# Keeping q, k and v of a sequence in SBUF, with the projection weights streamed from DRAM: a transformer layer on eight cores

## The reference

```python
x = x + _layernorm(attn(_layernorm(x), cos, sin, wq, bq, wk, wv, bv, wo, bo))
x = x + _layernorm(ffn(_layernorm(x), w1, conv_w, conv_b, w2))

# attn: 16 heads of 64
q = x @ wq + bq;  k = x @ wk;  v = x @ wv + bv
q, k = rope of the last 1024 tokens of q and k, in bfloat16
out = softmax(q k^T / 8) v;  return out @ wo + bo
# ffn: hidden size 4096, weights quantized to -1, 0, 1 and activations to 8 bits
h = bit_linear(x, w1); h = silu(depthwise_conv(h, conv_w) + conv_b); return bit_linear(h, w2)
```

## Time and profile before

| | |
|---|---|
| timed runs | 5171.26 and 5133.98 us, median 5152.62 |
| profiled execution | 5104.38 us |
| its span on the slowest core (core 7) | 5102.8 us, 42393 instructions |
| spans of the 8 cores | 5071.9 to 5102.8 us |
| mean granted TensorE clock, by core | 0.826 to 0.829 |
| busy share of the span | PE 58%, weight loads 21%, DVE 40%, ACT 38%, POOL 3% |
| DMA | 343.42 MB, mean 67 GB/s |

### The profile page before, as it was taken

One profiled execution on the slowest core, in us unless ns is written; L12 is line 12 of the kernel. 1 busy time (PEld: TensorE's weight loads), 2 busy tenths in 40 slices (PEclk: granted clock), 3 DMA queues, 4 the chain that ended last, 5 costly groups with the idle time before them and its releaser, 6 DMA issues. The chain is left out here.

```text
span 5102.8 us, 42393 instructions; the slowest of 8 cores (5071.9 to 5102.8 us)
## 1 busy us (share of the span) xinstructions
PE 2950.4 (58%) x12366; PEld 1065.1 (21%) x12366; DVE 2023.0 (40%) x3238; ACT 1943.1 (38%) x2427; POOL 139.3 (3%) x246
## 2 busy tenths in 40 slices
PE   0000456678876331455788886331887788177577
PEld 0000222112211111222112211110332333033233
DVE  3334311244545444222244545444444344343433
ACT  0001344767775122344767765111222122242422
POOL 0000000000000000000000000000000000100000
PEclk9999988888987665788778888665998899588788
DMA  8574000100000222100100000223111111423232
GB/s 260 194 251 135 32 38 38 50 15 30 15 17 2 76 66 79 38 37 32 44 15 29 15 17 3 67 76 124 42 50 42 62 47 49 144 75 109 90 116 70
DMA packets 140105, 343.42 MB, mean 67 GB/s; under 512 B 42405, under 2 KB 75237, under 8 KB 135782
## 3 DMA queue, kind: packets, MB, share of 16 engines
q1 hardware_dynamic: 108330, 206.18, 12.1%
q0 software_dynamic: 31552, 134.53, 7.8%
HBM read 218.87 MB, written 117.60 MB: 66 GB/s over the span
## 5 line engine op out<-in xcount | busy, mean ns | idle before, releaser
L692 ACT ACTIVATE ptil<-sc,negM 128x1024 bf16<-128x1024 f32 x1024 | 1054.8, 1142 | 366.0 <-PE sc L623 365.1
L703 PE MATMUL accA<-ptil,dch 128*65 128x512 bf16 x1024 | 453.2, 443 | 154.9 <-DVE tmpB L722 153.9
L620 PE MATMUL sc<-qch,kch 64*128 64x512 bf16 x1024 | 423.5, 414 | 71.1 <-DMA dch<-vd_sp 24.5
L623 PE MATMUL sc<-qch,kch 64*128 64x512 bf16 x1024 | 434.0, 424 | 0.0
L705 PE MATMUL accB<-ptil,dch 128*65 128x512 bf16 x1024 | 430.6, 421 | 0.0
L1172 PE MATMUL p2a<-w2q,ring 128*128 128x512 bf16 x1024 | 241.1, 399 | 184.1 <-DVE outt L1189 159.0
L715 DVE COPY lbufA<-accA 1x512 f32<-1x512 f32 x64 | 43.8, 685 | 633.2 <-PE accB L705 633.2
L998 ACT ACTIVATE hsb<-pcA,convb_s 128x512 bf16<-128x512 f32 x128 | 88.0, 687 | 519.6 <-PE pcA L989 513.9
L157 ACT ACTIVATE stat<-stat 128x1 f32<-128x1 f32 x128 | 25.9, 203 | 675.7 <-DVE stat L152 675.6
L965 PE MATMUL pwA<-xqd,w1q 128*128 128x512 bf16 x1024 | 245.1, 382 | 44.6 <-DVE hsc L974 44.6
L861 PE MATMUL pw<-ident,xqtm 128*128 128x128 bf16 x256 | 32.4, 307 | 390.3 <-DVE xqtm L852 390.3
(11 more groups left out here) (215 smaller groups left out, 4557.2 us busy)
## 6 DMA issues: line engine op xcount, KB each, us to landing
xr<-x SPq DMA_DIRECT2D x64, 512.0 KB, 4.7
hs_sp<-hsb SPq DMA_DIRECT2D x64, 512.0 KB, 2.6
ring<-hs_sp SPq DMA_DIRECT2D x8, 4096.0 KB, 16.3
wstg<-w1t SPq DMA_DIRECT2D x4, 4096.0 KB, 15.9
wstg<-w1t POOLq DMA_DIRECT2D x4, 4096.0 KB, 24.5
wstg<-w2t SPq DMA_DIRECT2D x4, 4096.0 KB, 18.9
wstg<-w2t POOLq DMA_DIRECT2D x4, 4096.0 KB, 28.3
x_sp<-x2t SPq DMA_DIRECT2D x32, 512.0 KB, 2.7
```

Source lines behind the costliest of these rows:

```text
L620: TE.matmul(sc[sl][:, 0:512], kc_[0:64, kt * 128:(kt + 1) * 128], qc_[0:64, qc * 512:(qc + 1) * 512], start=True, stop=True, tile_position ...
L623: smmv[g] = st.inc(TE.matmul(sc[sl][:, 512:1024], kc_[64:128, kt * 128:(kt + 1) * 128], qc_[64:128, qc * 512:(qc + 1) * 512], start=True, ...
L692: expv[pl] = ss.inc(S.activation(ptil[pl][:], sc[sl][:], AF.Exp, bias=negM[:, p:p + 1], scale=1.0))
L703: TE.matmul(accA[:], dc4[:, kt, 0:65], ptil[pl][:, 0:512], start=(kt == 0), stop=(kt == NKT - 1))
```

## The change

The attention stage no longer reads q, k and v from DRAM. They stay in SBUF for a whole sequence (`qres`, `kres`, `vres`, 32 KB + 32 KB + 32.5 KB per partition), and ACT, DVE and rope write there directly. The three DRAM buffers, the seven spills of each block, the waits for them at its end and the loads in the attention stage are gone.

The space comes from three places. `w3` (48 KB per partition) is gone: in the setup DVE casts each batch of wq, wk and wv into `wqa` or `wqb`, and G spills it with four DMAs to `wqkv_sp`, which is laid out by column block; from there the QKV stage loads the weights of one block (768 KB) at a time into `wsb0` and `wsb1`, the next block's at the start of each block. The staging buffers are half as wide, so `quant_weight` makes 8 batches of 2 MB of each pass. In the Wo stage `ln3t`, `ln2t`, `qx16` and `xqtm` have one buffer each. The `xr` buffers are allocated per stage, as many as are used.

```diff
+    wqkv_sp = nc.dram_tensor("wqkv_sp", [OC, 128, 3 * KC * 128], BF16,
+                             kind="Internal").ap()
-        w3 = w3_es.enter_context(nc.sbuf_tensor(_un("w3"), [128, 3 * KC * H], BF16))
+        qres = w3_es.enter_context(nc.sbuf_tensor(_un("qres"), [128, OC * T], BF16))
+        kres = w3_es.enter_context(nc.sbuf_tensor(_un("kres"), [128, OC * T], BF16))
+        vres = w3_es.enter_context(
+            nc.sbuf_tensor(_un("vres"), [128, NPAIR * NKT * 130], BF16))
...
-        wstg0 = _ph.enter_context(nc.sbuf_tensor(_un("wstg0"), [128, 2 * DH], F32))
+        wstg0 = _ph.enter_context(nc.sbuf_tensor(_un("wstg0"), [128, DH], F32))
...
                 dstg[i % 2].wait(V, lv)
+                if i >= 2:
+                    dss[i % 2].wait(V, wspill[i % 2])
                 castv.append(sv.inc(V.tensor_copy(
-                    w3[:, (wh * KC + b * 4) * H:(wh * KC + b * 4 + 4) * H],
-                    stg[i % 2][:, 0:4 * H])))
+                    wqx[i % 2][:, 0:4 * H], stg[i % 2][:, 0:4 * H])))
+                sv.wait(G, castv[-1])
+                for k4 in range(4):
+                    tix = wh * KC + b * 4 + k4
+                    wspill[i % 2] = dss[i % 2].inc(G.dma_start(
+                        wqkv_sp[:, :, tix * 128:(tix + 1) * 128].rearrange(
+                            "o p n -> p o n"),
+                        wqx[i % 2][:, k4 * H:(k4 + 1) * H].rearrange(
+                            "p (o n) -> p o n", n=128)), 16)
...
-                nb = 2 * DH // width
+                nb = DH // width
...
+                    wldv[0] = dstg[0].inc(SY.dma_start(wsb[0][:], wqkv_sp[0]), 16)
                     for oc in range(OC):
                         par = oc % 2
-                        if oc >= 2:
-                            dsq[par].wait(S, spq[par])
-                            dsk[par].wait(S, spk[par])
-                            dsd[par].wait(V, spd[par])
+                        if oc + 1 < OC:
+                            sl2 = (oc + 1) % 2
+                            eng = SY if sl2 == 0 else G
+                            st.wait(eng, wsuse[sl2])
+                            wldv[sl2] = dstg[sl2].inc(
+                                eng.dma_start(wsb[sl2][:], wqkv_sp[oc + 1]), 16)
+                        dstg[par].wait(TE, wldv[par])
...
                             rolast = sv.inc(V.tensor_tensor(
-                                ro[:, ridx * 512:(ridx + 1) * 512], rt1[:], rt2[:],
-                                op=OP.add))
+                                src, rt1[:], rt2[:], op=OP.add))
...
-                        dsq[par].inc(G.dma_start(qf_sp[s, oc][:, 0:1024], qcb[par][:, 0:1024]), 16)
...
-                        spd[par] = dsd[par].inc(G.dma_start(vd_sp[s, oc], db[par][:]), 16)
-                        if oc < OC - 1:
-                            dsq[par].wait(V, spq[par])
-                            dsk[par].wait(V, spk[par])
-                            dsq[par].wait(S, spq[par])
-                            dsk[par].wait(S, spk[par])
...
-                    datt[0].inc(G.dma_start(qch[0][:], qf_sp[s, 0]), 16)
-                    datt[0].inc(G.dma_start(kch[0][:], kf_sp[s, 0]), 16)
-                    ld[0] = datt[0].inc(G.dma_start(dch[0][:], vd_sp[s, 0]), 16)
...
-                    datt[0].wait(TE, ld[0])
...
-                            sv.wait(S, ln3use[i % 2])
-                            l3v = ss.inc(S.activation(ln3t[i % 2][:], pw[i][:],
+                            sv.wait(S, ln3use_s)
+                            l3v = ss.inc(S.activation(ln3t[:], pw[i][:],
...
-                            sv.wait(S, ln2use[i % 2])
-                            l2v = ss.inc(S.activation(ln2t[i % 2][:], x2t[i][:],
+                            sv.wait(S, ln2use_s)
+                            l2v = ss.inc(S.activation(ln2t[:], x2t[i][:],
...
-                            st.wait(V, xqtmuse[i % 2])
+                            st.wait(V, xqtmuse_s)
```

More of the change, by code:

```diff
@@ L333, in build_nc @@
                 _ph = ExitStack()
+                xr = [_ph.enter_context(nc.sbuf_tensor(_un("xra"), [128, H], F32))
+                      for _ in range(3)]
                 ln1b0 = _ph.enter_context(nc.sbuf_tensor(_un("ln1b0"), [128, H], BF16))
@@ L395, in build_nc @@
                 with _ph:
[L396 to L405, removed]
+                    wsb = [wsb0, wsb1]
+                    if s == 0:
+                        VR = vres[:, :].rearrange("p (t c) -> p t c", c=130)
+                        V.memset(VR[:, :, 64:65], 1.0)
+                        onesv = sv.inc(V.memset(VR[:, :, 129:130], 1.0))
+                    else:
+                        onesv = 0
                     evq = evk = evv = 0
@@ L451, in build_nc @@
                             sv.wait(TE, trv)
-                            sv.wait(TE, onesv)
+                            if s == 0:
+                                sv.wait(TE, onesv)
                             for i4 in range(4):
@@ L586, in build_nc @@
                 with _ph:
-                    qch, kch, dch = [qch0, qch1], [kch0, kch1], [dch0, dch1]
                     ptil = [ptil0, ptil1, ptil2]
@@ L734, in build_nc @@
                 _ph = ExitStack()
-                ln3t = [_ph.enter_context(nc.sbuf_tensor(_un("ln3t"), [128, H], F32))
-                        for _ in range(2)]
+                xr = [_ph.enter_context(nc.sbuf_tensor(_un("xrb"), [128, H], F32))
+                      for _ in range(4)]
+                ln3t = _ph.enter_context(nc.sbuf_tensor(_un("ln3t"), [128, H], F32))
                 x2t = [_ph.enter_context(nc.sbuf_tensor(_un("x2t"), [128, H], F32))
                        for _ in range(4)]
-                ln2t = [_ph.enter_context(nc.sbuf_tensor(_un("ln2t"), [128, H], F32))
-                        for _ in range(2)]
-                qx16 = [_ph.enter_context(nc.sbuf_tensor(_un("qx16"), [128, H], F16))
-                        for _ in range(2)]
-                xqtm = [_ph.enter_context(nc.sbuf_tensor(_un("xqtm"), [128, H], BF16))
-                        for _ in range(2)]
+                ln2t = _ph.enter_context(nc.sbuf_tensor(_un("ln2t"), [128, H], F32))
+                qx16 = _ph.enter_context(nc.sbuf_tensor(_un("qx16"), [128, H], F16))
+                xqtm = _ph.enter_context(nc.sbuf_tensor(_un("xqtm"), [128, H], BF16))
                 xqs0 = _ph.enter_context(nc.sbuf_tensor(_un("xqs0"), [128, 512], BF16))
@@ L846, in build_nc @@
                             sv.wait(V)
-                            st.wait(V, xqtmuse[i % 2])
-                            sv.inc(V.tensor_scalar(qx16[i % 2][:], ln2t[i % 2][:],
+                            st.wait(V, xqtmuse_s)
+                            sv.inc(V.tensor_scalar(qx16[:], ln2t[:],
                                                    stat[:, qo + 3:qo + 4], RM,
@@ L852, in build_nc @@
                             xqv = sv.inc(V.tensor_scalar(
-                                xqtm[i % 2][:], qx16[i % 2][:], -RM, None,
+                                xqtm[:], qx16[:], -RM, None,
                                 op0=OP.add))
-                            ln2use[i % 2] = xqv
+                            ln2use_s = xqv
                             sv.wait(TE, xqv)
```

129 lines of the change are left out of this document (50 added, 79 removed).

## The result

| | before | after |
|---|---|---|
| median of the timed runs | 5126.32 us (19 runs) | 5170.38 us (20 runs) |
| span of the profiled execution, slowest core | 5102.8 us | 5157.2 us |
| spans of the 8 cores | 5071.9 to 5102.8 us | 5130.6 to 5157.2 us |
| DMA | 343.42 MB | 311.67 MB |

The ratio after / before is 1.0086, with an interval of 1.0056 to 1.0117: 44 us slower (29 to 60). Ratios here leave out the runs that a lower clock on one die disturbed, the medians do not, so the two need not agree to the last digit.

A forecast was written before the change was run, and what follows sets the result against it. Bounds differ by stage: setup DMA-bound with holes, QKV and Wo chains between engines, attention mostly ACT. Terms 50 - 10 + 12 + 0 - 23 + 23 = +52 us on 5136.5 gave about 5188 us, range 5135 to 5270.

The forecast's parts named there:

- A: Setup, wq to wo: loads queued behind spills on G, casts in pairs and 256-byte pieces cost +50 us (39 to 87).
- B: Setup, w1 and w2: half-size batches shorten first passes and tail, lengthen second passes; -10 us (-25 to +10).
- C: QKV start: PE waits 5.8 us a stage for its first weights after the barrier; +12 us (10 to 15).
- D: QKV block ends: the removed spills and their waits were hidden behind PE's matmuls; 0 us.
- E: Attention start: the wait for the first loads goes away in both sequences; -23 us (-20 to -25).
- F: Wo stage: with one `ln3t`, ACT and DVE alternate instead of overlapping; +23 us (18 to 24), other single buffers 0.
- rival 2: QKV block ends: spill waits did cost, up to 3.7 us at 14 boundaries, -52 us, so not slower; chance 0.06.
- rival 3: Attention: an earlier start keeps PE at a higher clock, -160 us, so over 2% faster; chance 0.03.

The follow-up runs named there:

- b2: Kernel before with staging buffers and weight batches half as wide, nothing else; 5097.83 us, ratio 0.9975 to the kernel before.
- c2: Changed kernel with all setup spills on ACT's queue, no `ln3t`, first QKV weights loaded ahead of layer norm 1; 5007.22 us, ratio 0.9779 to the kernel before.
- a5: Changed kernel with all setup spills (wq, wk, wv and quantized w1, w2) issued from ACT's queue; 5067.02 us, ratio 0.9926 to the kernel before.
- b3: Kernel before without the spill waits at a column block's end, `ro` given a second buffer; 5136.54 us, ratio 1.0026 to the kernel before.
- b1: Kernel before with one `ln3t` buffer instead of two, nothing else; 5169.79 us, ratio 1.0091 to the kernel before.
- a4: Changed kernel with the load of batch i + 1 issued on G ahead of batch i's spills; 5142.28 us, ratio 1.0056 to the kernel before.
- a2: Changed kernel with the spills of wq, wk and wv issued from ACT's queue instead of G's; ratio 1.0084 to the kernel before.
- a1: Changed kernel with the same spilled bytes in 2 KB rows instead of 256-byte pieces, weights misordered; 5148.16 us, ratio 1.0061 to the kernel before.
- c1: Kernel before with the spills of quantized w1 and w2 on ACT's queue and no `ln3t`; 5041.61 us, ratio 0.9846 to the kernel before.
- a3: Changed kernel without `ln3t`, ACT writing into `x2t[i]` and DVE adding in place; profiled execution 32.9 us shorter than the changed kernel's.

## Why the prediction was right, point by point

The forecast was +52 us on the profiled execution, and its cores became 53.7 us longer in the mean (the slowest one 54.4). The forecast of the time, 5188, lies 18 us above the median of 5170.38, and 10 of these come from its base: it was taken as 5136.5 from three executions, and 19 give 5126.32. The sum was right as a whole; term by term it was not.

| part | forecast | measured |
|---|---|---|
| A, wq to wo | +50 (39 to 87) | +51.3 |
| B, half-size batches | -10 (-25 to +10) | -2.3 in b2, +3.5 in the changed kernel, neither clear of the spread of that row |
| C, first QKV weights | +12 (10 to 15) | +8.1 up to the first QKV matmuls; +5.8 by the stages, 9.0 by c2 against a5 |
| D, spill waits | 0 (-52) | no gain in b3 |
| E, first loads of attention | -23 (-25 to -20) | -22.3 in the waits, -26.9 with the stages |
| F, one `ln3t` | +23 (18 to 24) | +21.1; alone +23.3 in b1 |

**A was right, and by its mechanism.** DVE and the queues of the changed kernel in the setup (timeline):

```profile
17.94 2.29 DVE L230 CAST wqa<-wstg 128x4096 bf16<-128x4096 f32 x1 [2.82 <-DMA wstg<-wq]
20.86 3.74 POOL L235 DMA_DIRECT2D wqkv_sp<-wqa  x4 [16.97 <-DVE wqa L230]
...
40.66 2.29 DVE L230 CAST wqb<-wstg 128x4096 bf16<-128x4096 f32 x1 [20.43 <-DMA wstg<-wq]
42.87 2.29 DVE L230 CAST wqa<-wstg 128x4096 bf16<-128x4096 f32 x1
43.49 4.77 POOL L235 DMA_DIRECT2D wqkv_sp<-wqb  x4 [18.14 <-DVE wqb L230]
...
48.25 3.51 POOL L235 DMA_DIRECT2D wqkv_sp<-wqa  x4
51.75 0.76 POOL L223 DMA_DIRECT2D wstg<-wk  x1
69.83 2.29 DVE L230 CAST wqb<-wstg 128x4096 bf16<-128x4096 f32 x1 [24.68 <-DMA wstg<-wk]
...
100.38 2.29 DVE L230 CAST wqb<-wstg 128x4096 bf16<-128x4096 f32 x1 [26.05 <-DMA wstg<-wv]
...
121.53 2.29 DVE L249 CAST wo<-wstg 128x4096 bf16<-128x4096 f32 x1 [16.66 <-DMA wstg<-wo]
```

The first cast ends at 20.23 (forecast 21), casts come in pairs, the pairs stand 69.83 - 40.66 = 29.17 and 30.55 us apart (29.3), and the last cast ends at 123.82 (121). a4 confirmed the order as the cause of 20.2 us of it, and a2 the shared queue, order included, as the cause of 31.7; a1 gave 8.7 to the piece size. The price that the sum gave the 256-byte data (4.6 us a batch in place of 2.7) is not confirmed by this: a1 took 8.7 us off instead of the 11 of that difference, and in it the issues on G, which the sum left out but for the last one, became shorter too. One detail was wrong and cost nothing: the spill of a pair's first batch was to be issued only after the second cast, but it starts at 43.49, beside that cast, and is only longer for it. The Trainium skill (DMA: Bandwidth & Descriptors, Specifications) wants at least 512 B per transfer, since less means a read-modify-write. The direction agrees with a1, but a doubling would have made a batch 2.7 us dearer, and a1 shows 1.45, with the shorter issues in it.

**B had one term mis-sized.** The first passes (-7 each) and the tail (-4) came as forecast: -7.3, -6.4 and -3.5 in b2. The second passes were given +4 each, from "two more starts of 2 us". They cost 7.9 and 7.0 in b2 and 10.5 and 9.0 in the changed kernel: a round that is added costs about 4 us, not 2. The step took only the start of a load for the price of a round. In the rows of a5's section a round is DVE's work on a pair (28.94 - 18.98 = 10 us), and then the load wait of 18.98 us, of which two transfers at 319 GB/s are 13.2: in the other 5.8 us lie the late issue of G's load, its start and completion, and the spills beside the loads. How these 5.8 divide was not measured. Whether B as a whole gained or lost is open: over the kernels of each kind the second row of the table reads 379.3 us in the mean with large batches (before, b1, b3) and 381.4 with small ones, and 378.1 in b2. What the sum never priced is how much of both passes hangs on G's queue: with the spills on ACT the second passes are 35 and 39 us shorter in the changed kernel (a5) and 25 and 27 us in the kernel before (c1).

**C was too large, for a reason that the trace before would have shown.** PE's first QKV matmul behind the barrier, in the changed kernel and then in c2, where the weights are there already:

```profile
625.14 3.57 PE L433 MATMUL pq<-attA,wsb 128*128 128x512 bf16 x8 [5.80 <-DMA wsb<-wqkv_sp]
```

```profile
513.67 3.57 PE L434 MATMUL pq<-attA,wsb 128*128 128x512 bf16 x8 [1.54 <-PEq L143]
```

The forecast of a wait of 5.8 us was exact. But 1.5 of it is the barrier, which PE waited for before as well. The change costs 5.80 - 1.54 = 4.3 us a stage, 8.6 in all. Over all cores the time from the first x load to the first QKV matmul grew by 3.8 and 4.3 us, 8.1 in all. The stages give only 5.8 because the second QKV stage is 3.0 us shorter (350.5 to 347.5 us), in every kernel with the changed QKV stage, and only in the second sequence. There PE also no longer waits for the column of ones in v; that this is the cause was not tested. The forecast had no such term.

**D was right.** b3 has no wait at a block's end and is not faster; rival 2 is refuted.

**E was right in the waits.** The stages' ends and PE's first scores in both sequences:

```profile
976.79 0.17 DVE L562 COPY negM<-pbc 128x8 f32<-128x8 f32 x1 [0.81 <-PE pbc L559]
...
977.28 0.58 PE L609 MATMUL sc<-qres,kres 64*128 64x512 bf16 x1 [0.59 <-PEq L143]
...
2510.31 0.58 PE L609 MATMUL sc<-qres,kres 64*128 64x512 bf16 x1 [0.59 <-PEq L143]
```

0.49 us instead of the 11.2 of the earlier trace rows, and an idle time of 0.59 instead of 13.16. The 13.16 is that of the slowest core; in the mean of the cores the wait between the last QKV instruction and the first scores fell by 11.2 and 11.1 us, together -22.3. The stages themselves moved by +4.5 and -9.1, but kernels with the same attention differ as much (the first stage takes 753.1 to 766.3 us in the six without loads). With loads (before, b1, b2, c1) both stages with their waits take 1539.3 us in the mean, without (after, a1, a2, a3, a5, c2) 1516.4, which is -22.9. Rival 3 wanted 160 us from the clock; the granted clock of the stage went from 0.85 to 0.83 in the first sequence. On average the first stage is 4 us longer in the kernels without loads, and the second 4 us shorter than the wait explains. This goes with the clock. The prediction held against rival 3 that both stages lie within 1 us of each other; on the core that it read they do not (from the first scores to the issue of the last store, core 7 of the kernel before, columns as in the earlier trace rows):

```profile
918.00:1668.00 750.00, 575.83 (x2176) 144.63 (x2176) 351.97 (x272) 527.78 (x513) 9.40 (x18) 0.85 0.05 17
2439.50:3207.60 768.10, 595.45 (x2176) 146.19 (x2176) 351.96 (x272) 529.63 (x513) 9.40 (x18) 0.82 0.05 16
```

Over the 160 attention stages of the ten profiled executions other than a4 and b3 the length runs from 743 us at a granted clock of 0.867 to 770 at 0.817, with loads or without (correlation -0.99). The mean clock of the two stages is 0.849 and 0.835 in the kernels with loads, 0.841 and 0.844 in those without, which is the +4 and the -4 us. So with the clock this stage varies by up to 27 us, more than the loads cost; rival 3 was refuted by the measured lengths and not by its argument. What sets the clock of a stage no run here shows.

**F was right.** All 32 instances of L774 on the slowest core of the changed kernel (idle time of its engine, and what ended it):

```profile
L774 ACT ACTIVATE ln3t<-pw,stat x32: 1204/1204/1205, 1767.0 to 3528.5; 128x1024 f32<-128x1024 f32 x32
...
  DVE x2t L781: 37.5, 24
...
L798 ACT ACTIVATE ln2t<-x2t,stat x32: 1239/1251/1252, 1786.7 to 3560.5; 128x1024 f32<-128x1024 f32 x32
...
  DVE stat L163: 1.4, 8
```

24 waits are three a group, as forecast, and `ln2t`, now single too, never waits for its reader. b1 has the one edit alone and the same length, so the single `ln2t`, `qx16` and `xqtm` cost nothing that shows.

So B came out 8 to 14 us dearer, C 3 to 6 cheaper, and E some 4 better, by the granted clock of two stages and not by the loads. Errors of this size cancelled, which is luck, and the +52 is closer to the +54 than its terms deserve.

## What to carry to other kernels

A queue issues in program order, so a load that stands behind a store of data still being computed waits for the computation: list for each DMA what is issued ahead of it on its queue and when that becomes ready (issuing the load first took 20 of the 51 us that the change had cost in the first part of the setup, moving the stores to another queue 32 of them, and 35 and 39 us off two later passes). The attention stage, with a DMA share of 0.06, gained only the wait for its first load when its loads went away, though the kernel moves 32 MB less. When a wait is added behind a barrier, subtract the barrier's own wait that stood there before. When two kernels' stages differ by a few us, compare their granted clocks first.

## What the runs showed of the hardware that was not expected

- **Issuing many pieces from ACT's queue.** The first four issues of 1024 pieces took 17.79 us on ACT's queue and the next four 3.72 (a2, above); on G's queue four took 3.74 or 3.51. Of the 17.79 us one issue, the third, took 13.74. The same happened in the next two pairs of batches (third issue 13.97 and 13.94 us), each time beside a 2 MB load that SyncE issued at the same moment, and never in the group behind; what holds the issue was not separated. The spills that were to be taken off the critical queue became what DVE waited for.
- **Issue time on G follows the number of pieces.** Four issues took 2.33 us with 128 pieces of 2 KB each (a1) and 3.74 us with 1024 pieces of 256 bytes each; a single undisturbed one 0.54 and 0.89 us.
- **A DVE cast beside an issue on G makes it longer, by little.** 4.77 us with the cast of 42.87 to 45.16 beside it and 3.51 us without. The first of the four issues takes all of it: 2.14 us, from 43.49 to 45.63, just behind the cast's end; in a1 it takes 1.78 us and ends at 46.31, 0.1 us behind its cast. The Trainium skill (SBUF — State Buffer, SBUF: two separate sides) tells that some DVE operations lock GpSimd out of a shared port, so that a DMA issued there waits for its descriptors, and advises the ACT or SP queue. The longer issue agrees with the lock. The advice paid for the spills of w1 and w2 (a5) and for those of wq to wv (a2, 31.7 us), with the order in the queue in both gains, though ACT's queue was held for the 17.79 us above.
